# One long run of 64x64 pieces: P times V leaves the score banks so that the next scores can follow it

## The reference

```python
def _ln(x, g, b):
    m = jnp.mean(x, axis=-1, keepdims=True)
    v = jnp.var(x, axis=-1, keepdims=True)
    return (x - m) * jax.lax.rsqrt(v + EPS) * g + b

def _attn(xq, xc, Wq, Wk, Wv, Wo, bo):
    q = (xq @ Wq).reshape(B, N, HEADS, D_HEAD)
    k = (xc @ Wk).reshape(B, S, HEADS, D_HEAD)
    v = (xc @ Wv).reshape(B, S, HEADS, D_HEAD)
    scores = jnp.einsum('bnhd,bshd->bhns', q, k) * D_HEAD ** (-0.5)
    attn = jax.nn.softmax(scores, axis=-1)
    out = jnp.einsum('bhns,bshd->bnhd', attn, v).reshape(B, N, HEADS * D_HEAD)
    return out @ Wo + bo

x = _attn(_ln(x, g1, b1), _ln(x, g1, b1), Wq1, Wk1, Wv1, Wo1, bo1) + x      # SELF
x = _attn(_ln(x, g2, b2), context, Wq2, Wk2, Wv2, Wo2, bo2) + x             # CROSS
x = _geglu_ff(_ln(x, g3, b3), Wp, bp, Wf, bf) + x                           # GEGLU
# then block two: x + (out + ffn(layernorm(out))), out = cross attention (16 heads of 8)  # CROSS2, FFN
```

## Time and profile before

| | |
|---|---|
| median of three runs | 463.44 us |
| the profiled execution's own time | 461.13 us |
| its span (first to last instruction) | 459.4 us |
| PE busy | 440.3 us, 96% |
| DVE, ACT, POOL busy | 357.1, 318.8, 196.2 us |
| PE's granted clock, mean | 0.996 |

### The profile page before, as it was taken

How to read it: one execution, slowest core, us unless ns; L and a number is a source line. 1 busy time by engine, 2 the same in 40 slices (tenths; PEclk the granted TensorE clock), 3 DMA queues, 4 the chain that set the end, 5 groups by cost and what they waited for, 6 DMA issues and landing times.

```text
span 459.4 us, 17514 instructions
## 1 busy us (share of the span) xinstructions
PE 440.3 (96%) x7564; PEld 405.7 (88%) x7564; DVE 357.1 (78%) x656; ACT 318.8 (69%) x586; POOL 196.2 (43%) x217
## 2 busy tenths in 40 slices
PE   7999999799999999999989999979999999999897
PEld 7979999698999999999979999878999778777797
DVE  5878888588797897887968878876874778888572
ACT  5686686577778768778776787655455576776763
POOL 2783243355355535654344343411432232132583
PEclk9999999999999999999999999989999999999999
DMA  7102021210200000000000000000000000000011
GB/s 227 55 2 83 10 76 3 76 47 4 62 3 12 6 8 10 3 11 10 4 11 1 13 10 3 4 1 2 1 0 17 12 10 21 0 1 1 11 37 46
DMA packets 17301, 10.56 MB, mean 23 GB/s; under 512 B 7889, under 2 KB 16273, under 8 KB 17233
## 3 DMA queue, kind: packets, MB, share of 16 engines
q1 hardware_dynamic: 16800, 9.48, 7.3%
q10 hardware_dynamic: 432, 0.07, 0.2%
HBM read 8.50 MB, written 1.05 MB: 21 GB/s over the span
## 4 chain that ended last, share of the span: by engine, by line
PE 85%; DVE 8%; ACT 4%; issue 2%; DMA 1%; POOL 0%; DVEq 0%; ACTq 0%; POOLq 0%
PE stage L610 12%; PE stage L611 11%; PE stage L612 11%; PE scp L782 7%; PE scp L703 6%; PE scp L928 6%; PE scp L752 6%; PE out0p L802 4%; PE out0p L803 3%; PE out0p L828 3%; PE out0p L804 3%; PE stage L766 2%; PE scp L720 2%; DVE pr L1230 1%; DVE mx L1225 1%
## 5 line engine op out<-in xcount | busy, mean ns | idle before, releaser
L1483 POOL TENSOR_TENSOR pr<-pr,rc 128x1024 f32<-128x1024 f32 x31 | 58.4, 1903 | 76.1 <-DVE rc L1260 76.0
L1015 ACT ACTIVATE pr<-pr 128x1024 f32<-128x1024 f32 x48 | 50.9, 1059 | 38.7 <-DVE pr L1230 30.9
L1424 POOL TENSOR_TENSOR rstd<-veps,neghalf 128x2 f32<-128x2 f32 x32 | 22.7, 711 | 88.5 <-DVE veps L1178 88.4
L953 ACT ACTIVATE vt<-stage 64x512 f32<-64x512 f32 x81 | 48.0, 592 | 4.8 <-PE stage L612 1.2
L1273 DVE COPY vt<-stage 64x512 f32<-64x512 f32 x47 | 32.6, 694 | 21.7 <-PE stage L612 20.7
L1225 DVE TENSOR_REDUCE mx<-scp 128x16 f32<-128x1024 f32 x32 | 39.2, 1224 | 9.1 <-PE scp L703 8.7
L953 ACT ACTIVATE ot_h<-scp 128x512 fp32r<-128x512 f32 x64 | 33.3, 602 | 16.4 <-PE scp L782 16.4
L1279 DVE TENSOR_TENSOR ot_r<-scp,ot_h 128x512 fp32r<-128x512 f32 x64 | 39.9, 683 | 5.2 <-ACT ot_h L953 3.7
L953 ACT ACTIVATE k_of_heads<-stage 128x512 f32<-128x512 f32 x62 | 36.9, 597 | 5.4
L1230 DVE TENSOR_TENSOR pr<-scp,mx 128x1024 f32<-128x1024 f32 x32 | 39.2, 1224 | 1.1
L782 PE MATMUL scp<-pt,vt 64*64 64x64 f32 x2048 | 34.4, 220 | 4.7 <-issue 4.3
(11 more groups left out here) (256 smaller groups left out, 1414.1 us busy)
## 6 DMA issues: line engine op xcount, KB each, us to landing
ctx_in<-in_ctx_dram SPq DMA_DIRECT2D x16, 96.0 KB, 2.0
masked_k<-in_L_xattn_Wo_dram SPq DMA_DIRECT2D x2, 512.0 KB, 3.8
out_dram<-rows SPq DMA_DIRECT2D x8, 128.0 KB, 1.8
rows<-in_x_dram SPq DMA_DIRECT2D x1, 768.0 KB, 9.4
pr<-in_L_xattn_Wq_dram SPq DMA_DIRECT2D x1, 512.0 KB, 4.4
pr<-in_L_xattn_Wk_dram SPq DMA_DIRECT2D x1, 512.0 KB, 6.3
pt<-in_L_xattn_Wv_dram SPq DMA_DIRECT2D x1, 512.0 KB, 7.6
rows<-in_L_xattn_Wq_dram SPq DMA_DIRECT2D x1, 512.0 KB, 3.7
```

Of the source, the lines that this page charges most:

```text
L953: return nc.scalar.activation(dst, s, ACT.Copy)
L1015: nc.scalar.activation(pr[t][:, :], pr[t][:, :], ACT.Exp, scale=scale[s.phase]).then_inc(exped, 1)
L1483: nc.gpsimd.tensor_tensor(halves(pr[t][:, :]), halves(pr[t][:, :]), rc[:, t, :, None].to_broadcast([ROWS, H, N]), ALU.mult).then_inc(probs, 1)
```

## The change

It does three things in SELF and CROSS. P times V no longer goes to `scp` but to the three `stage` banks (products 0 to 2) and to `out0p` (product 3), except in the last group of CROSS. The scores of the next group stand directly behind P times V, and the V products behind the scores. The waits follow: `av_step` waits for its `stage` banks and, for `out0p`, until the output of the group before has been added; the scores wait for the copies of `pt` instead of those of P times V; `out_step` waits for all four products of P times V. On DVE the copy of the first V product moves behind the first maximum and subtraction of the softmax.

```diff
@@ Counts.use @@
-        if kind != "av":
+        if kind != "av" or ((p, g) != (CROSS, GROUPS - 1) and i < 3):
             self.uses.append((kind, p, g, i))
@@ Counts.group @@
             if one.phase != GEGLU:
-                self.vals(one.phase, one.first, range(3))
                 for t in range(T):
                     self.softmax(one.phase, one.first, t)
+                self.vals(one.phase, one.first, range(3))
...
+        def av_bank(s, u):
+
+            if s.is_group(CROSS, GROUPS - 1):
+                return scp[:, u, :]
+            return out0p if u == 3 else stage[cnt.bank("av", s, u)]
+
         def av_copy(s, u):
             t, i = divmod(u, 2)
-            return ot_h[:, :, i, t, :], scp[:, 2 * t + i, :].rearrange("p (m n) -> p m n", m=PAIRS // 2)
+            return ot_h[:, :, i, t, :], av_bank(s, u)[:, :].rearrange("p (m n) -> p m n", m=PAIRS // 2)
@@ scores_step @@
                 if before:
-                    pe.wait_ge(dve, cnt.at("dve", before, 2 * t + 1, kind="av"))
+                    pe.wait_ge(pt_act, cnt.at("pt_act", before, t, 0))
+                    pe.wait_ge(pt_dve, cnt.at("pt_dve", before, t))
@@ av_step @@
-                banks = [scp[:, 2 * t + i, :] for i in range(2)]
+                banks = [av_bank(s, 2 * t + i) for i in range(2)]
+                for u in range(2 * t, 2 * t + 2):
+                    if ("av", s.phase, s.first, u) in cnt.uses:
+                        stage_for(s, "av", s, u)
+                if t == 1 and s.before() and not s.is_group(CROSS, GROUPS - 1):
+                    pe.wait_ge(added, cnt.at("added", s.before()))
@@ out_step @@
-                pe.wait_ge(dve, cnt.at("dve", s, 2 + i, kind="av"))
+                pe.wait_ge(dve, cnt.at("dve", s, 2 + i if s.is_group(CROSS, GROUPS - 1) else 3, kind="av"))
@@ group, tensor @@
-                    val_step(one, range(3), s)
                     scores_step(one, 0)
                     scores_step(one, 1)
+                    val_step(one, range(3), s)
@@ group, vector @@
-                    val_step(one, (0,))
                     max_step(one, 0)
                     shift_step(one, 0)
+                    val_step(one, (0,))
```

## The result

The changed kernel takes 480.53 us (median of four runs, 479.05 to 483.48) against 463.38 before. The ratio is 1.0375, 95% interval 1.0323 to 1.0427: slower. The forecast was 477.4, range 467 to 486. The profiled execution took 479.05 us, its span is 477.3, 17.9 longer than before.

The account below looks back on a forecast made before the run. PE was taken to bound the kernel, busy 440.3 of 459.4 us. Terms -5.0 + 15.4 - 1.9 + 6.0 - 0.5 = +14.0 on 463.44 gave 477.4 us, range 467 to 486.

Parts of the forecast that it names:

- The mechanism: PE's program arrives in 256-instruction blocks; each merged run of 64x64 pieces holds two edges, so PE stops at the second.
- Rivals 2 and 3: 2: blocks asked for early enough, 462.0 us, chance 0.05; 3: neither stalls nor rests, only the switch, 456.0 us, chance 0.05.
- rival 1: Instructions stall as forecast, but the chain of rests through ACT and POOL is hidden; 471.4 us, chance 0.18.
- Rival 4: Stalls in merged runs worse, blocks hindering each other or meeting weight loads: 1.7 us a group, 486 us, chance 0.10.
- The size of the stall: In each merged run PE stops 3.0 - 1.88 = 1.1 us; 14 of them, +15.4 us (10 to 20).
- The old stalls: Two of three existing PE stalls in 64x64 pieces go, 1.4 and 0.5 us: -1.9 us; the 3.10 us one stays.
- The switch: PE changing between 128x128 and 64x64 matmuls: merging runs saves 0.36 us per group, 14 groups, -5.0 us.
- the 88 waits: PE's added waits, taken by its sequencer ahead of the pieces: taken as 0, at most 4 us if none hidden.
- The rests: `proj_step` waits for POOL's rest of the context, behind later V products, in SELF 6, 7, CROSS 0 to 5: +6.0 us.
- CROSS 6: Bound by DVE: PE's 2.5 us wait for the `vt` copy shortens as sums come 0.5 earlier; -0.5 us.
- The other waits: New waits for `stage` banks, `added` and copies of the P times V products: cost nothing, 0 us.

Follow-up runs that it names:

- `half_scores`: `round_first_lean` with half of the scores left out (pairs 4 to 7 of every group but the first); one execution, 455.25 us.
- `round_first_lean`: `round_first` without the waits in av_step and the scores that the two pt waits already cover; 471.49 us, ratio 1.0201 to the kernel before.
- `round_first`: The changed kernel with ACT's rounding of src and ctx_src ahead of its copies of the three V products; 475.49 us, ratio 1.0269 to the kernel before.
- `banks_only`: The changed kernel with V products again between P times V and the scores, new banks and waits kept; 468.24 us, ratio 1.0111 to the kernel before.
- four variants: Kernel before with 9, 37 or 13 idle matmuls added, and the last with CROSS 6's second V copy moved earlier; 460.6, 467.89, 459.26, 459.37 us.

## Why the prediction was right

**The mechanism** was as put: a wait without releaser in every merged run, 256 instructions behind another edge, shown by the counts in the changed kernel, by the packets of q8, by the moved edges and by `half_scores`. Rivals 2 and 3 fall with that, and rival 1 with the 8 waits for POOL. Rival 4 holds in part: where three edges come in quick order the last block took longer (3.6 us in SELF 4, 4.1 in CROSS 5), but the average of 1.3 stayed below its 1.7.

The Trainium skill, "Runtime: NRT & Kernel Launch", section "Instruction fetch mechanics", gives TensorE a store of 2048 instructions. No run here bears that out: with eight blocks ahead, the stalls above one block behind an edge would not be there. The 16 KiB blocks of 256 instructions that it states are what every count here shows.

**The size of the stall** was the term mis-sized. The rows give 17.3 + 0.7 + 0.7 = 18.7 us of idle time, and with 0.21 each for the modelled ends 22.3 us for 17 stalls, 1.3 each. I had 14 of 1.1. Two things were missed. I counted edges inside the runs and not one lying 5 instructions ahead of one: in SELF 4 and CROSS 5 it makes three edges in quick order, and these are the two stalls in P times V. And the block took 3.3 us from edge to use on average, where the middle of my bounds was 3.0, while PE spent 2.0 us and not 1.88 on the 256 instructions; the single stalls go from 0.9 to 2.2.

**The old stalls.** I took the two short ones off and left the 3.10 us as it was. It went as well: SELF 3 has one stall of 2.17 now, which is among the 17. By starts the three old ones were 4.58 + 3 x 0.21 = 5.2 us, so -5.2 and not -1.9. That I had left 3.3 us of gain out was luck for the number: it took back more than half of what the stalls were short.

**The switch** was priced at 0.36 us a group. SELF 5 took 19.01, and less its stall of 0.93 it is 18.08 against 18.34 of the same group before: 0.26. The group of `round_first_lean` makes 18.02, 0.32. So the price of the switch was near right, and the part on the 88 waits was wrong: I took them at nothing, and with most of them gone P times V is 0.1 us shorter. Over the 14 groups SELF 0 to CROSS 5, less their stalls, before takes 256.1 us and `round_first`, which has no waits for the rests, 252.6: -3.5 in place of -5.0.

**The rests**: 8 waits, together 4.4 us idle; with the modelled end and the restart of the matmul 0.8 each, 6.3 us, where 6.0 stood. `round_first` removed all of them.

**CROSS 6**: 19.11 against 20.07 us before, 1.0 less, where I had 0.5. PE's wait fell from 2.5 to 1.3, and the granted clock was 1.00 in the window of CROSS 6 above, where the window of before has 0.91:

```profile
290.02:310.09 20.07, 17.55 (x345) 16.12 (x344) 16.90 (x27) 11.87 (x21) 5.29 (x6) 0.91 0.01 3
```

A mean of 0.91 is a stretch at the lower level of 1.2 GHz behind the wait of 2.5 us; behind the one of 1.3 us PE stayed at 2.4 GHz. That is the profiled execution alone: in the other three of the changed kernel the mean granted clock was 0.989 to 0.996, so there it did fall somewhere, and they are 1.0 to 4.4 us longer. With as many matmuls PE was busy 1.02 us less, 16.53 for 17.55, part of it the switch.

**Sum by what was measured**: 22.3 - 5.2 = 17.1, of which 1.1 in CROSS 6 lies inside its wait: 16.0; + 6.3 - 3.5 - 1.0 = 17.8, against 17.9 of span and 17.2 between the medians. The forecast of +14.0 was 3.8 us low against this sum: 2.5 by the stalls (the new ones 5.8 longer than forecast, the old ones 3.3 more to take off), 1.5 by the switch and the waits, 0.3 by the rests, less 0.5 by CROSS 6. The mechanism and its places were right; that the number came within 0.7% owes something to two misses of opposite sign.

**The other waits** (banks, `added`, the fourth subtraction) hold PE nowhere, as argued: no row of PE names them. `banks_only` shows how near that was: with the V products one run earlier, 14 of them waited for a bank.

## What to carry to other kernels

When many short matmuls are lined up, count instructions, not only microseconds: here each block of 256 took 2.6 to 4.1 us from edge to use, and a run that uses up a block in 1.9 us stops at its second edge, whatever was saved on the switch. Slow matmuls between two runs of small ones are not a loss, they are the time in which the next block comes. And a wait with "issue" as its releaser that comes in multiples of 256 instructions is no matter of data; look for the packet of the instruction queue ahead of it. A few idle instructions in a place where the engine waits anyway can move it, here for 0.5%, but it may come back elsewhere.

## What the runs showed of the hardware

- Blocks of PE's program: from an edge to the use of the next block 2.6 us (no stall) to 4.1 us (the stall of 2.17 us in SELF 3), 3.3 on average at the stalls of the merged runs. Of these 3.3, 0.9 pass before the packet of q8 starts, 1.1 are the packet, and 1.4 pass from its end to PE's next instruction.
- Beside a load of 512 KB the block came later: in the kernel before and its four variants the packet started 2.7 to 3.8 us behind the edge, at all their other stalls 0.3 to 1.6, and PE had it 5.1 to 6.1 us behind the edge. The stall was 3.3 us with 2.8 us of work between the edges and 0.9 to 1.6 with 4.2.
- Standalone waits in front of 64x64 pieces: P times V takes 2.01 us in `round_first`, which has six of them (three ahead of each half), and 1.92 in `round_first_lean`, which has two. In SELF 0, with five, it takes 1.90 in `round_first` and 1.97 in the changed kernel, so the price of one is not shown.
- 18 matmuls of 64x64 at the cold start, all into one region of PSUM, took 2.2 us (0.12 each), where in a warm run over four tile positions one takes 0.015.
